# VectorE makes the first half of the projection's lower part in the half groups

## The reference

```python
for e in range(E):                                   # E = 8
    h = gelu(flat_x @ w_fc[e])                       # 256 -> 1024
    out = out + combine[:, e:e+1] * (h @ w_proj[e])  # 1024 -> 256
```

## Time and profile before

| | us |
|---|---|
| median of 3 runs | 658.87 |
| profiled execution, its time | 659.68 |
| profiled execution, its span | 657.8 |
| PE busy | 607.8 (92%) |
| DVE busy | 486.7 (74%) |
| ACT busy | 416.1 (63%) |
| POOL busy | 386.9 (59%) |
| granted TensorE clock, mean | 0.99 |

### The profile page before, as it was taken

How to read it: one execution, slowest core, us unless ns; L and a number is a source line. 1 busy time by engine, 2 the same in 40 slices (tenths; PEclk the granted TensorE clock), 3 DMA queues, 4 the chain that set the end, 5 groups by cost and what they waited for, 6 DMA issues and landing times. The chain is left out here.

```text
span 657.8 us, 15198 instructions
## 1 busy us (share of the span) xinstructions
PE 607.8 (92%) x4726; PEld 580.6 (88%) x4726; DVE 486.7 (74%) x1164; ACT 416.1 (63%) x732; POOL 386.9 (59%) x282
## 2 busy tenths in 40 slices
PE   1798999999988959999999999999999999999993
PEld 1697888888778959989999999999999999999983
DVE  7757668789788957667887778778788687867671
ACT  2814576766679747787756657566565665656660
POOL 5101111676675873556676676666767667688883
PEclk9999999999999979999999999999999999999998
DMA  8900010234588982853222131231312313121211
GB/s 344 306 31 1 22 44 33 83 115 153 194 295 290 264 221 51 272 168 60 35 51 46 32 64 33 49 48 32 64 34 44 54 32 62 28 43 25 34 25 16
DMA packets 37596, 62.47 MB, mean 95 GB/s; under 512 B 3696, under 2 KB 32944, under 8 KB 36400
## 3 DMA queue, kind: packets, MB, share of 16 engines
q1 hardware_dynamic: 16448, 36.19, 16.5%
q0 software_dynamic: 13296, 18.00, 15.1%
q10 hardware_dynamic: 7808, 7.74, 4.5%
HBM read 37.02 MB, written 24.89 MB: 94 GB/s over the span
## 5 line engine op out<-in xcount | busy, mean ns | idle before, releaser
L713 POOL TENSOR_TENSOR pj_lo<-w_ffn,pj_hi 128x1024 fp32r<-128x1024 f32 x66 | 163.2, 2476 | 88.1 <-ACT pj_hi L777 87.5
L1684 DVE TENSOR_TENSOR fc_lo<-w_ffn,fc_hi 128x1024 fp32r<-128x1024 f32 x78 | 113.6, 1489 | 55.7 <-ACT fc_hi L777 52.5
L702 POOL DMA_INDIRECT out<-y,add_id x71 | 111.4, 1569 | 46.3 <-issue 39.8
L777 ACT ACTIVATE pj_hi<-w_ffn 128x1024 fp32r x78 | 82.7, 1060 | 82.5 <-PE psO L2108 64.5
L2108 PE MATMUL psP<-pj_hi,h_hi 128*128 128x256 f32 x312 | 93.2, 299 | 6.7 <-DVE h_lo L1684 6.5
L777 ACT ACTIVATE fc_hi<-w_ffn 128x1024 fp32r x78 | 79.0, 1052 | 18.6 <-issue 18.6
L2108 PE MATMUL psP<-pj_lo,h_hi 128*128 128x256 f32 x312 | 88.3, 283 | 0.0
L2108 PE MATMUL psP<-pj_hi,h_lo 128*128 128x256 f32 x312 | 88.0, 282 | 0.0
L664 POOL DMA_INDIRECT slots<-rows,slot x64 | 67.8, 1059 | 21.8 <-issue 17.0
L2108 PE MATMUL psO<-pj_hi,h_hi 128*128 128x256 f32 x256 | 72.7, 284 | 0.0
L2108 PE MATMUL psO<-pj_lo,h_hi 128*128 128x256 f32 x256 | 72.5, 283 | 0.0
(11 more groups left out here) (365 smaller groups left out, 1610.4 us busy)
## 6 DMA issues: line engine op xcount, KB each, us to landing
w_ffn<-in_w_ffn SPq DMA_DIRECT2D x8, 2048.0 KB, 9.5
xg<-slots ACTq DMA_DIRECT2D x25, 265.0 KB, 2.9
xc<-in_x_ch SPq DMA_DIRECT2D x4, 1024.0 KB, 8.6
out<-x SPq DMA_DIRECT2D x16, 256.0 KB, 2.2
x<-in_x_tok SPq DMA_DIRECT2D x1, 3072.0 KB, 24.7
slots<-fill SPq DMA_DIRECT2D x9, 265.0 KB, 10.7
xg<-slots SPq DMA_DIRECT2D x7, 265.0 KB, 5.4
out<-y,add_id POOLq DMA_INDIRECT x71
```

The source lines that it names most:

```text
L702: nc.gpsimd.indirect_dma_start(out_d, bass.IndirectOffsetOnAxis(ap=add_id[:, s:s + 1], axis=0), y[:, s, :], None, compute_op=ALU.add).then ...
L713: nc.gpsimd.tensor_tensor(pj_lo[:, 4 * a:4 * a + 4, :], w_ffn[:, bass.ds(e, 1), (2 + a) * DFF:(3 + a) * DFF].rearrange("p a (c d) -> p (a ...
L777: nc.scalar.activation(out, src, ACT.Copy, **kw).then_inc(done, 1)
L1684: v.tensor_tensor(out, whole, upper.bitcast(F32), ALU.subtract).then_inc(done, 1)
```

## The change

In groups 32 to 38 POOL's `proj_lower` is called for a = 1 only, and DVE calls its own `proj_lower` for a = 0 as the first step of the group, ahead of `hidden(g, 0)`. DVE's function loads the expert's number into a register again, waits for `pj_hi` a = 0 of the group, and subtracts. No other order, buffer or semaphore is changed; `down` waits for the same two semaphores.

```diff
@@ -733,7 +733,7 @@
                 proj_lower(g)
                 add(g - 1)
             for g in range(FULL, GROUPS):
-                proj_lower(g)
+                proj_lower(g, range(1, 2))
                 add(g - 1)
             add(GROUPS - 1)
 
@@ -1787,6 +1787,7 @@
                     fc_lower(g + 1, 1 - par, expert_of(g + 1))
                     behind(g)
                 elif is_half(g):
+                    proj_lower(g, range(0, 1))
                     hidden(g, 0)
                     if g_on(g + 1):
                         slot_meta(g + 1)
```

## The result

| | before | after |
|---|---|---|
| median of 6 runs, us | 658.73 | 653.0 (651.09 to 653.59) |
| ratio to before | | 0.9902, 95% interval 0.9884 to 0.992 |
| profiled execution, its time | 659.68 | 653.59 |
| profiled execution, its span | 657.8 | 651.1 |

The change makes the kernel 1.0% faster, 5.7 us between the medians; 5.2 us was forecast.

A forecast was written before the change was run, and what follows sets the result against it. No engine was full; a loop of waits, with DVE's `fc_lo` slowed by POOL's subtractions, set the 9.49 us beat. Gains of 4.15 + 1.04 = 5.2 us from 658.87 gave 653.7 us, range 651.8 to 656.6.

The forecast's parts named there:

- The added step is free: DVE's `pj_lo` of 1.22 us fits its 1.49 us idle stretch before chunk 0's cast, leaving 0.34 us (cover).
- The first `fc_lo` takes 1.22 instead of 2.05: On DVE in groups 33 to 37, no longer held by POOL: 0.83 us gained per group.
- the first rival: DVE's added register load isn't hidden, or a small slip: 0.6 gained per group, 655.2 us in total; chance 0.19.
- POOL's margin: POOL's subtraction ends 0.19 us ahead of `fc_lo`; its tiny copy after that was taken to cost nothing.
- the third rival: Nothing is freed: POOL still lies on `fc_lo` or the loop closes elsewhere; 0 to 1 us, 658.4; chance 0.08.
- Why the later one waits: DVE and POOL instructions that both read these tiles don't run together; the slow `fc_lo` ended 1.09 us after POOL.
- What is late next: DVE's chain of 7.18 us plus 1.48 us of PE and ACT becomes the loop: a beat of 8.66 us.
- PE alone would do 8.45, as group 32 shows: Group 32's 8.45 us was taken as PE's own beat in the half groups.
- the upper bound of the gain: For groups 33 to 37, PE's own beat as limit: 47.47 - 5 x 8.45 = 5.2 us.
- The end of the last group: POOL free 1.15 us earlier, DMA lands sooner, `y` follows PE's last matmul ("PE is last"): 1.04 us gained.
- The sum: 4.15 us from groups 33 to 37 plus 1.04 us at the end: 5.2 us.
- POOL first (the slower rival): POOL's subtraction starts before DVE's `pj_lo`, which waits: 2.1 us lost per group, 668.3 us in total; chance 0.06.

The follow-up runs named there:

- e1: Changed kernel, but in the half groups no engine makes `pj_lo` a = 0 and `down` doesn't wait for it; ratio to before 0.991.
- e8: Changed kernel with DVE's register loads early from group 34 on and POOL's tiny copy ahead of its subtraction there; ratio to before 0.9917.
- e2: Kernel before, plus one more DVE subtraction of the same shape ahead of `hidden(g, 0)` from group 33 on; 665.94 against 659.49 us, ratio 1.009.
- e4: Changed kernel with DVE's two register loads for the next group moved ahead of `hidden(g, 0)`; 656.46 us, ratio to before 0.9952.
- e7: Changed kernel with DVE's register loads early from group 33 on, group 32 left alone; 651.54 us, ratio to before 0.9892.
- e3: Changed kernel with DVE's `pj_lo` behind `hidden(g, 0)` instead of ahead of it; 660.76 against 659.49 us before, ratio 1.0013.
- e6: Changed kernel with DVE making the second half too, behind `hidden(g, 0)`, and POOL none in the half groups; 657.78 us, ratio to before 0.9997.
- e9: Changed kernel with the same split between DVE and POOL in the full groups 8 to 31 too; 653.19 us, ratio to before 0.9918.

## Why the prediction was right, step by step

- The added step is free: right. It lasts 1.22 us with no gap before it, 0.35 us of cover are left (0.34 forecast), and e1 without it is no faster. In group 34 the cover is 0.17, in 35 there is none.
- The first `fc_lo` takes 1.22 instead of 2.05: right in groups 33, 34, 36 and 37. Group 35 had a small slip, of the kind put with the first rival: ACT's `pj_hi` came late, `pj_lo` on DVE stood 0.35 us for it, `fc_lo` took 1.30 and the beat was 8.73. It is there in all three profiles of the changed kernel, so it is not chance; why ACT is late there I didn't settle. Group 34's `pj_lo`, some 0.17 us late, had its `pj_hi` 0.55 us before; that may be a register load not wholly hidden, which is the first rival's own mechanism, at a size that cost nothing. It is in all three profiles too, and no run tells its cause.
- POOL's margin: in groups 33, 36 and 37 POOL ends 0.22 or 0.23 us before `fc_lo` (0.19 forecast), and the copy got in between, as taken. In group 34 the margin is 0.03 us and `fc_lo` still takes 1.22; in 35 POOL ends 0.21 us after `fc_lo` is issued. So the third rival was right that it is thin, and right in its own objection: an overlap costs only its own length. e8, where `fc_lo` is issued 1.03 us before POOL's end, shows what a lost margin costs.
- Why the later one waits: the rule was put too narrowly, as holding for instructions "that both read these tiles". The tiny copy of the earlier trace rows reads `slot_id`, no tile of the subtraction, and waited for DVE all the same; e2's step writes into `h_hi`.
- What is late next: DVE's loop of 8.66 us; measured 8.64 to 8.67 in four groups. That this is DVE's and not PE's is shown by e4 and e7, where beats of 8.40 to 8.44 occur, and by the 3.24 us from the end of the first `fc_lo` to the next `up`, which hold in every kernel here. Wrong was "PE alone would do 8.45, as group 32 shows": group 32's beat is set by its first `fc_lo` too (5.22 + 3.23 us), and 8.40 occurs. The error moved the upper bound of the gain by 0.25 us and nothing else.
- The end of the last group: 1.04 forecast, 0.98 measured. "PE is last" was wrong by a hair: POOL issues the DMA 1.19 us earlier after the start of `up` (1.15 forecast), but the DMA takes 3.78 us instead of 3.56 and lands 0.09 after PE's end.
- The sum: 4.15 + 1.04 forecast, 4.12 + 0.98 measured.
- POOL first (the slower rival): it did not happen, and e2 shows that the order would have been real. What decides is whether POOL asks while DVE's `fc_lo` is still running. In group 33 POOL starts 1.04 us after `pj_lo` (591.06 and 590.02; 1.03 forecast) and 0.95 us after the end of `fc_lo`, in groups 34 and 35 0.87 and 0.98 us after `pj_lo`.

The range, 651.8 to 656.6, holds the median of 653.0. The trace accounts for 5.1 of the 5.7 us between the medians; the other 0.6 are not explained by the change and lie within the wandering of the stages before group 8, which I had not weighed. In the three profiles of the changed kernel that wandering is 2 us, over a third of the effect, so the total alone could not have confirmed the forecast to half a microsecond; the beats do.

## What to carry to other kernels

An engine that is only 74% busy, or 59%, can still set the beat if two of them keep each other waiting: compare the duration of one instruction shape in different groups of the same loop, and ask what ran beside the slow one. Moving work from one of the two to the other pays if it goes into a hole that is longer than the work and if it asks first; the same step a few instructions later (e3), or one step more (e6), gives the whole gain back. And it pays only in stages where the engine that does the main work waits (e9).

## What was not expected of the hardware

- When DVE and POOL both want to run such an instruction, the one that waits already is served, even if the other engine's next instruction is right behind. It holds both ways: in e2 DVE's step waits for POOL (3.41 us instead of 1.22), and in the kernel before POOL's tiny copy, right behind its own subtraction, waits for the `fc_lo` that was there first (1.19 us instead of 0.18).
- The instruction with which POOL issues an indirect DMA waits for a DVE subtraction that is already running, and only for that one. Alone it takes 1.57 us. At 594.39 `fc_lo` has 0.52 us left to run and it takes 1.97; in e9 (594.93) 0.93 are left and it takes 2.38; in e4 (591.56) 1.13 are left and it takes 2.56, although a second subtraction follows on DVE until 593.82. It is longer each time by what was left, less 0.12 to 0.14 us. A subtraction that starts behind it doesn't hold it up, nor is it held up, even if it starts only 0.05 us later. Timelines of POOL and of DVE of e6, group 33:

```profile
592.86 1.57 POOL L702 DMA_INDIRECT out<-y,add_id  x1 [1.48 <-ACT y L945]
...
592.91 1.23 DVE L1683 TENSOR_TENSOR pj_lo<-w_ffn,pj_hi 128x1024 fp32r<-128x1024 f32 x1 [0.35 <-issue]
```

  The Trainium skill ("SBUF — State Buffer", Who interferes with whom) says, as inferred, that `tensor_tensor` doesn't stall a DMA's descriptors, since it takes only the read side of the shared ports. The profile doesn't show the descriptors themselves, but e6 agrees: DVE's subtraction covers 1.23 of the 1.57 us and adds nothing. What waits is the start of the instruction.
- Register loads of an engine seem to run under its previous instruction; the profile doesn't show them, so this is read from the gaps. DVE stands 0.42 to 0.59 us ahead of `slot_w` and of `fc_lo`, behind instructions of 0.14 to 0.42 us. With the loads moved under `pj_lo` (e4) the gap ahead of `slot_w` is gone, and behind an instruction of 1.2 us or more there is none in most places (e3). Single places fall out of this by 0.17 to 0.40 us in most of the kernels (group 34 of the changed kernel, of e2 and of e3, group 33 of e9), and no run tells why.
